# Slot order in the second attention, its closing gate, and the first projections of a two-layer kernel

## The reference, cut to what matters

```
x = x + L0_xattn(layernorm(x), ctx)      # 8 heads of 8, band of 64, softmax, relu(out) * ctx, w_ct
x = x + L0_ffn(layernorm(x))             # top half of the 64 rows by x @ w_r, gelu, scattered back
x = x + L1_xattn(layernorm(x), ctx, ctx) # 32 query heads on 8 key groups, softmax, Wfc, bfc
x = x + L1_ffn(layernorm(x))             # square(relu(h @ up)) @ down + (h @ expert) * sum(top-2 of h @ gate)
                                         # then layernorm with gamma and beta
```

## Time and profile before

| what | us |
| --- | --- |
| median of 3 runs | 335.25 |
| lowest, highest | 334.99, 337.39 |
| the profiled execution, its own time | 335.92 |
| its span, first to last instruction | 334.2 |
| PE busy in the span | 309.2 (93%) |
| DVE busy | 237.7 (71%) |
| ACT busy | 198.6 (59%) |
| POOL busy | 181.4 (54%) |

### The profile page before, as it was taken

The page is one execution under the profiler, slowest core; times in us unless marked ns, Lnnn a source line. Parts: engine busy times, 40 slices in busy tenths (PEclk is TensorE's granted clock), DMA queues, the critical chain, the costliest instruction groups (busy, mean ns, idle before and its releaser), DMA issues.

```text
span 334.2 us, 7216 instructions
## 1 busy us (share of the span) xinstructions
PE 309.2 (93%) x2178; PEld 241.2 (72%) x2178; DVE 237.7 (71%) x921; ACT 198.6 (59%) x415; POOL 181.4 (54%) x294
## 2 busy tenths in 40 slices
PE   6997989998999999999998998879899999999992
PEld 4976667676777777776687875657666578888892
DVE  6778889999999999984246156755788647662264
ACT  4758988887777787868531324566678944104210
POOL 6648566677776957577514414243443831336643
PEclk9999999999999999999999999999999999999999
DMA  6999020202010101100000000000000000000000
GB/s 194 365 372 341 8 49 2 50 1 49 3 41 8 38 13 28 26 1 3 2 0 0 2 0 0 0 2 1 2 1 2 0 2 0 3 32 15 19 31 31
DMA packets 13302, 14.51 MB, mean 43 GB/s; under 512 B 2513, under 2 KB 11985, under 8 KB 13265
## 3 DMA queue, kind: packets, MB, share of 16 engines
q1 hardware_dynamic: 12688, 13.72, 13.0%
q10 hardware_dynamic: 576, 0.33, 0.3%
HBM read 10.64 MB, written 1.05 MB: 35 GB/s over the span
## 4 chain that ended last, share of the span: by engine, by line
PE 61%; POOL 13%; DVE 11%; issue 8%; ACT 6%; POOLq 0%; DVEq 0%; ACTq 0%
PE S L772 6%; PE S L432 5%; PE O L459 5%; PE ST L443 4%; PE ST L797 4%; PE S L566 4%; PE S L648 2%; PE S L715 2%; POOL rstd L1081 2%; POOL hT L1097 2%; PE PJ L692 2%; DVE masked L1294 2%; PE O L729 2%; PE PJ L395 2%; PE O L597 2%
## 5 line engine op out<-in xcount | busy, mean ns | idle before, releaser
L1294 DVE CUSTOM_DVE_ANT_0 masked<-S,band 128x192 bf16<-128x192 f32 x256 | 79.6, 353 | 8.9 <-PE S L432 6.9
L893 ACT ACTIVATE ex<-ST 128x384 f32<-128x384 f32 x128 | 60.9, 491 | 17.7 <-PE ST L443 16.3
L1078 POOL TENSOR_SCALAR rstd<-mv 128x1 f32<-128x1 f32 x40 | 12.1, 303 | 76.1 <-DVE mv L1231 75.5
L432 PE MATMUL S<-qk 128*128 128x384 f32 x128 | 52.1, 408 | 0.8 <-DVE mw L1294 0.4
L443 PE MATMUL ST<-qk 128*128 128x192 f32 x256 | 48.1, 271 | 2.5 <-ACT ex L893 2.0
L443 PEld LDWEIGHTS ST<-qk 128*128 128x128 f32 x256 | 44.9, 189 | 5.0 <-issue 4.4
L1138 POOL TENSOR_SCALAR_AFFINE_SELECT ex<-ex 128x512 f32<-128x512 f32 x32 | 20.4, 639 | 29.6 <-ACT ex L893 29.5
L459 PE MATMUL O<-ex,v 128*32 128x192 f32 x512 | 34.1, 338 | 0.0
L432 PEld LDWEIGHTS S<-qk 128*128 128x128 f32 x128 | 24.1, 188 | 13.3 <-issue 11.4
L1426 DVE TENSOR_REDUCE mw<-S 128x8 f32<-128x512 f32 x32 | 22.0, 686 | 13.0 <-PE S L648 13.0
L863 ACT ACTIVATE hs<-PJ,sb,byhead 128x512 fp32r<-128x512 f32 x29 | 22.6, 779 | 11.5 <-PE PJ L396 10.6
(11 more groups left out here) (204 smaller groups left out, 720.6 us busy)
## 6 DMA issues: line engine op xcount, KB each, us to landing
qk<-kp SPq DMA_DIRECT2D x48, 48.0 KB
w<-in_w SPq DMA_DIRECT2D x2, 1024.0 KB, 10.0
cx<-in_cx SPq DMA_DIRECT2D x1, 1024.0 KB, 9.7
up<-in_up SPq DMA_DIRECT2D x1, 1024.0 KB, 11.8
down<-in_down SPq DMA_DIRECT2D x1, 1024.0 KB, 10.9
out<-x SPq DMA_DIRECT2D x8, 128.0 KB, 1.7
cxT<-in_cxT SPq DMA_DIRECT2D x1, 768.0 KB, 6.1
x<-in_x SPq DMA_DIRECT2D x1, 768.0 KB, 7.9
```

The source lines that it names most:

```text
L432: mm(out, r32(qp[:, t % 2, g, b, P * c:P * c + P]), r32(mv_), start=True, stop=True).then_inc(s["pe_s"], 1)
L893: A(ex[:, (n // 2) % 4, 2 * w:2 * w + 2, :], ST[n % 2][:, 0:2 * WIN].rearrange("p (h k) -> p h k", h=2), ACT.Exp, scale=SCALE).then_inc(s[ ...
L1294: last = V.tensor_tensor_reduce(out=masked[:, n % 2, h, :], in0=S[n % 2][:, WIN * h:WIN * h + WIN], in1=band[:, c, :], scale=1.0, scalar=N ...
```

## The change

Six things are moved or split. (1) Opening: `ctx_keys(0, 0)` goes behind the second projection, `ctx_keys(0, 1)` to slot 12 of the first sixteen; the second rounded copy of tile 0 is DVE's, and DVE makes the masks ahead of the normalising, the bias products with one instruction in place of four. (2) ACT's copies L1032 stand first in their slots, behind the gelu only. (3) `ffn_out(2)` and `ffn_out(3)` stand one slot sooner, in -5 and 3. (4) POOL's `x + beta` is made in slots 21, 25, ..., 49 into the buffer `cx`, which is free by then. (5) The top-two steps are a function `moe_gate`; for tiles 5 to 7 it runs inside `moe_out` of the tile before, ahead of its last instruction. (6) The semaphore `dve_xh` is new. The pieces of the diff follow in the order of the file: shared helpers, PE, ACT, POOL, DVE. The copies that are added near the start of ACT's `slot1` are taken out at its end.

```
+        def rounded(t, b):
+            if t == 0:
+                return s[("act_xh", "dve_xh")[b]], 1
+            return s["act_xh"], 2 * t + b
...
-        CTX_K = {8 - UNITS: (0, 1), 1: (1, 0), 2: (1, 1), 3: (2, 0), 4: (2, 1), 8: (3, 0), 10: (3, 1)}
+        CTX_K = {7 - UNITS: (0, 0), 12 - UNITS: (0, 1), 1: (1, 0), 2: (1, 1), 3: (2, 0), 4: (2, 1), 8: (3, 0), 10: (3, 1)}
...
                 if n == 0:
-                    pe.wait_ge(s["act_xh"], 2 * t + 2)
+                    for b in range(2):
+                        pe.wait_ge(*rounded(t, b))
                     pe.wait_ge(s["dve_xl"], t + 1)
...
             warm_up(3)
-            ctx_keys(0, 0)
             for T_, l in SLOTS_ALL:
...
-                    A(r32(xs[64:128, 1, :]), xn[64:128, t % 2, :], ACT.Copy).then_inc(s["act_xh"], 1)
+                    if t:
+                        A(r32(xs[64:128, 1, :]), xn[64:128, t % 2, :], ACT.Copy).then_inc(s["act_xh"], 1)
...
                 if n == 2:
                     A(warm[:, :], ident[:, 0:1], ACT.Exp)
+                for i in (0, 3):
+                    p = at(n, SPREAD[i] + 1, 8, PAIRS)
+                    if p is not None:
+                        act.wait_ge(s["gp_e"], 4 * p + i + 1)
+                        if p >= 3:
+                            act.wait_ge(s["gp_st"], 8 * (p - 2))
+                        A(stacked(p, i), S[1][:, :].rearrange("p (g t q) -> p g t q", g=2, t=4), ACT.Copy).then_inc(s["ga_q"], 1)
                 t = at(n, 10, 4, TILES)
...
...
+                t = at(n, 21, 4, TILES)
+                if t is not None:
+                    pool.wait_ge(s["g_x"], t + 1)
+                    G.tensor_tensor(cx[:, t, :], x[:, t, :], vecs[:, 4, :], ALU.add).then_inc(s["h_xb"], 1)
...
             def moe_norm(t):
-                pool.wait_ge(s["g_x"], t + 1)
-                if t == 0:
-                    pool.wait_ge(s["gp_bt"], TILES)
-                if t >= 2:
-                    pool.wait_ge(s["h_out"], t - 1)
-                G.tensor_tensor(on[:, t % 2, :], x[:, t, :], vecs[:, 4, :], ALU.add).then_inc(s["h_xb"], 1)
                 inv_std(t, "h_ln2", 2 * t + 2, "h_rstd2")
...
-            dve.wait_ge(s["pool_rstd"], 1)
-            normalise(xn[:, 0, :], 0, "dve_xn")
             dve.wait_ge(s["pe_part"], 1)
...
-            for n in range(4):
-                last = V.tensor_tensor(sb0[:, n:n + 1], b0[:, n:n + 1], part0[:, n // 2:n // 2 + 1], ALU.mult)
-            last.then_inc(s["dve_w"], 1)
+            V.tensor_tensor(sb0[:, :].rearrange("p (a b) -> p a b", a=2), b0.rearrange("p (a b) -> p a b", a=2),
+                            part0[:, :, None].to_broadcast([P, 2, 2]), ALU.mult).then_inc(s["dve_w"], 1)
+            dve.wait_ge(s["pool_rstd"], 1)
+            normalise(xn[:, 0, :], 0, "dve_xn")
+            dve.wait_ge(s["dve_xn"], 1)
+            V.tensor_copy(r32(xs[64:128, 1, :]), xn[64:128, 0, :]).then_inc(s["dve_xh"], 1)
...
-                c = at(n, -4, 8, 2)
+                c = at(n, -5, 8, 2)
                 if c is not None:
                     ffn_out(2 + c)
...
-            def moe_out(t):
+            def moe_gate(t):
                 dve.wait_ge(s["hp_eg"], t + 1)
...
+            def moe_out(t):
+                if t < 5:
+                    moe_gate(t)
                 dve.wait_ge(s["h_moe"], t + 1)
...
+                if 4 <= t < TILES - 1:
+                    moe_gate(t + 1)
                 dve.wait_ge(s["h_y"], 2 * t + 2)
...
-                V.scalar_tensor_tensor(out=x[:, t, :], in0=yr[:, 1, :], scalar=rstd[:, t:t + 1], in1=on[:, t % 2, :],
+                V.scalar_tensor_tensor(out=x[:, t, :], in0=yr[:, 1, :], scalar=rstd[:, t:t + 1], in1=cx[:, t, :],
```

More of the change, by code:

```diff
@@ L156, in build @@
                  "act_hs act_v act_mt act_exp act_o act_bt act_relu act_xh act_sb "
-                 "dve_w act_band dve_ln dve_xn dve_xl dve_mix dve_max dve_rc dve_on dve_x dve_zero "
+                 "dve_w act_band dve_ln dve_xn dve_xh dve_xl dve_mix dve_max dve_rc dve_on dve_x dve_zero "
                  "pool_var pool_rstd pool_mw pool_y pool_xn pool_fxn pool_half pool_kb pool_sel pool_zero act_kb ld_kb0 ld_kb1 dve_spread dve_masks dve_v1 ld_sel "
@@ L1025, in slot1 @@
                     nc.scalar.copy(onT[:, t % 2, :], XB[:, 0:T]).then_inc(s["ga_bt"], 1)
[L1026 to L1032, removed]
             def moe_relu(m):
@@ L1355, in slot_ @@
                 if l == (1 if T_ < 1 else 0) and 0 <= t < TILES:
-                    dve.wait_ge(s["act_xh"], 2 * t + 1)
+                    dve.wait_ge(*rounded(t, 0))
                     V.tensor_tensor(r32(xs[64:128, 0, :]), xn[0:64, t % 2, :], xs[0:64, 0, :], ALU.subtract)
                 if l == (2 if T_ < 1 else 1) and 0 <= t < TILES:
-                    dve.wait_ge(s["act_xh"], 2 * t + 2)
+                    dve.wait_ge(*rounded(t, 1))
                     V.tensor_tensor(r32(xs[0:64, 1, :]), xn[64:128, t % 2, :], xs[64:128, 1, :], ALU.subtract)\
```

## The result

The changed kernel takes 333.72 us (median of 6 runs, 333.59 to 333.91), the kernel before in the same comparison 335.88 us (6 runs, 334.99 to 337.39). The ratio is 0.993, with a 95% interval of 0.991 to 0.995: 0.7% faster, 2.2 us, where 3.95 us were forecast. The kernel before has a median of 335.88 us here and 335.25 us in the three runs on which the forecast of 331.3 us stands, so 0.6 us of the distance between 331.3 and 333.7 us is the starting point and not the change. The profiled execution took 333.68 us, with a span of 331.9 us and a granted clock of 0.997.

The account below looks back on a forecast made before the run. PE, busy 93% of the span, was taken as the bound, so only its waits count. Terms sum to -3.95 us: profiled execution 335.92 to 332.0 us, median 335.25 to 331.3 us (0.50); range 329.9 to 334.0 us.

Parts of the forecast that it names:

- -1.3, -1.5 and -1.1 us: Second attention: PE waits removed by `ffn_out(3)` in slot 3, then by group 0's copies at slots 10 and 18.
- `ffn_out(2)`: Slot -5: the sum delays DVE's copy of group 1, so PE waits 0.36 us and restarts, +0.6 us.
- the copy ahead of the rounding: ACT, slots -1, 7, 15: rounding, difference and maxima come later; +0.5 us at slot -1, +0.15 and 0 after.
- The close: Last tiles: top-two and scaling done earlier, so the last sum starts when PE's last product ends, -0.7 us.
- (a): Gains at slots 10 and 18 half return as waits for maxima or exponentials, 332.6 us; with (e) chance 0.22.
- (e): Group 0's late copy waits for PE's spreading, so slots 10 and 18 stay, 333.9 us; with (a) chance 0.22.
- Rival (c): Maxima become the bound: the swap costs 0.5 us in three slots, `ffn_out(2)` 0.6 to 1.2; 336.7 us, chance 0.04.
- POOL's additions in slots 21 to 49: Eight additions moved to where POOL is mostly idle and PE has next to no waits: cost 0.
- rival (d): POOL's additions lie on DVE's path, eight times 0.36 = 2.9 us at most, 334.2 us; chance 0.06.
- Slot 23: Last pair's group 3: the wait before the scores at 249.16 goes, some 0.3 us plus 0.24 restart, -0.5 us.
- The opening: First projection about a microsecond sooner at 8.84 us, but both key steps still precede the first scores: -0.1 us.
- Rival (b): The opening is worth its microsecond because a PE gap the chain doesn't show closes, 330.4 us; chance 0.13.

Follow-up runs that it names:

- the two kernels above: The kernel before with the opening's part alone, its doubled wait left out, 335.63 us; and the changed kernel with all parts, 333.72 us.

## Why the prediction was partly right

*What held.* PE is the bound, and what counts is where it stands still. The sizes from the profile were good: idle time plus 0.24 us of restart gave -1.3, -1.5 and -1.1 us, and -1.3, -1.6 and -1.1 were measured, the last two in the run with group 0's copies alone (`ffn_out(3)` in slot 3 had no run of its own; its -1.3 is that of the place in the trace). The two costs that speak against the change, +0.6 for `ffn_out(2)` and +0.5 for the copy ahead of the rounding, are there (1.0 of 1.1 us). The close gave its 0.7 us. Rivals (a) and (e) are refuted by the run with group 0's copies alone: nothing comes back, and the late copy moves. Rival (c) is refuted by the result itself; its swap of copy and rounding cost 0.4 us at slot -1, 0.1 at slot 7 and nothing at slot 15. The measured time, 333.7 us, is still inside the stated range (329.9 to 334.0), but near its end and close to the 333.9 us that stood for (a) and (e). That it lies inside is no merit of the terms: two costs of 1.7 us that the sum had at nothing took the place of two rivals that didn't happen, and "faster by more than 1%", to which I gave 0.52, didn't come true.

*The step that failed: "POOL's additions in slots 21 to 49 ... Cost 0".* They cost 0.9 us. The stretching was in the rows, and I let it go because PE has next to no waits behind 250 us in the trace of before. That premise was too kind: rows 2 leave out the smaller waits, and two of them lie there, one of 0.44 us at 262.44 for the very sum that the additions made late (L672 behind L1448). And a list of waits says how late DVE is, and not how much slack it has: PE came to the sum at 277.33 without a wait, but the sum had ended only 0.23 us before (276.69 and 0.41 us), so 0.54 us more of the square were 0.32 us of wait and a restart. It happened in two places of eight (0.32 and 0.27 us of wait, each with its restart), so rival (d) was the right mechanism at a third of its 2.9 us. The square (`relu(m) * relu(m)`) goes from 0.68 to 1.22 us beside one addition. The Trainium skill, "GPSIMD Engine Reference", section "Specifications", says that POOL shares its SBUF interfaces with VectorE, with contention where a VectorE instruction has two SBUF inputs; the trace agrees.

*The term that was missing: PE's second wait.* The sum holds nothing for the first attention. The diff puts two waits where one stood, and I took a wait that is already met for free. It costs about 0.15 us ahead of the first projection of each tile, 0.8 us in all.

*Slot 23, -0.5, measured -0.1.* The wait before the scores went; it was 0.24 us there, not the 0.3 of the mean. But the next thing late were the maxima of unit 23, which stand on DVE behind a normalising that takes 0.82 us beside an addition of POOL, as it did before the change, and PE waits 0.18 us for them:

```profile
245.11 0.74 POOL L1195 TENSOR_TENSOR yr<-x,vecs 128x256 f32<-128x256 f32 x1
245.18 0.82 DVE L1239 TENSOR_SCALAR xn<-x,mv,rstd 128x256 f32<-128x256 f32 x1 [0.41 <-POOL rstd L1088]
...
245.92 0.68 DVE L1432 TENSOR_REDUCE mw<-S 128x8 f32<-128x512 f32 x1
...
246.74 0.47 PE L654 MATMUL S<-qk 128*128 128x256 f32 x2 [0.18 <-DVE mw L1432]
```

Here I priced the wait and its restart, and didn't ask what is late next.

*The opening, -0.1.* The term was right (nothing, by the run with this part alone), and so was the reason, that both key steps stand ahead of the first scores in either order. The rest of the picture wasn't: moved, the keys leave PE idle before the projection, for 0.73 and 1.25 us in the two kernels above, which the forecast start at 8.84 didn't have. Rival (b) had it the wrong way round, since the keys filled that gap: with the keys behind, the projection starts 0.2 us after its last operand in each of the eight traces (8.60 to 8.98 us), so DVE's chain sets the start, and not PE. Whether a build with the keys in front and DVE's new order gains over the kernel before by itself was not run.

The two failures together, 1.7 us, are the whole difference between the 3.95 us forecast and the 2.3 us measured in the traces; the 0.4 us of slot 23 are balanced by small gains elsewhere.

## What to carry to other kernels

When PE is the bound and the edit is on another engine, read for each stretched or moved instruction how long before PE's arrival its consumer's input ends; "no wait there" can mean 0.2 us of slack. Count the waits that a helper emits inside a loop on the busiest engine, the ones already met too. Try each part of a bundle alone: here one piece (group 0's copies) gave at least as much as the whole, four cost time (the second wait, the additions, `ffn_out(2)`, group 3's copy ahead of the rounding), and two cured the same wait.

## What the runs showed of the hardware

- A wait on a semaphore that is already at its value wasn't free ahead of these matmuls: 0.15 us at each of tiles 2 to 7, 0.8 us in the first attention, in both directions. In all these places another operand, DVE's, ended only 0.10 to 0.25 us ahead of the matmul; what such a wait costs where all operands are long there was not measured.
- A POOL addition of 128x256 (0.79 us) that runs beside DVE's square of 128x512 stretches it from 0.68 to 1.22 us; beside a POOL addition the normalising of 128x256, which reads one tensor, goes from some 0.41 to 0.82 us.
- The matmuls on zeros in the opening take no fixed time: the six behind L604 (L611 after) ended between 7.35 and 8.84 us in these traces, with the same instructions. They start 0.43 us apart at first and 0.21 us apart later, and the step from the one to the other falls at another time in each execution: within the first of the six in the changed kernel's trace, behind all of them in the one before. The granted clock of the rows is 1.00 on either side.
- The first scores differ by up to 0.7 us between traces with the keys in front (12.72 to 13.46 us), as much as an edit of the opening can win. With the keys behind, they follow DVE's last operand (8.39 to 8.78 us) and not the matmuls on zeros: the trace in which these end first but one (7.57) has its first scores at 13.38, the one in which they end last (8.60) at 13.26.
